# Ternary weights in the convolution stage: the clamp on VectorE replaced by a sign on ScalarE

## The reference, cut to what matters

```
def weight_quant(w):
    s = 1.0 / jnp.clip(jnp.mean(jnp.abs(wf)), EPS, None)
    return (jnp.clip(jnp.round(wf * s), -1.0, 1.0) / s).astype(w.dtype)
```

```
kv = jnp.einsum('bhil,bhjl->bijhl', k_, v_)
y = irfft(rfft(kv, n=2L) * rfft(ssm_kernel, n=2L))[..., :L]
out = y + kv * D
out = jnp.einsum('bijhl,bhil->bjhl', out, q_)
```

## Time and profile before

| | us |
|---|---|
| median of 3 runs | 1134.99 (1133.25 to 1135.4) |
| the profiled execution's own time | 1131.52 |
| its span, first to last instruction | 1129.7 |
| PE busy | 955.3 (85%) |
| DVE busy | 796.1 (70%) |
| ACT busy | 635.8 (56%) |
| POOL busy | 529.4 (47%) |

### The profile page before, as it was taken

One profiled execution on the slowest core, in us unless ns is written; L12 is line 12 of the kernel. 1 busy time (PEld: TensorE's weight loads), 2 busy tenths in 40 slices (PEclk: granted clock), 3 DMA queues, 4 the chain that ended last, 5 costly groups with the idle time before them and its releaser, 6 DMA issues.

```text
span 1129.7 us, 15510 instructions
## 1 busy us (share of the span) xinstructions
PE 955.3 (85%) x5202; PEld 599.6 (53%) x5218; DVE 796.1 (70%) x1319; ACT 635.8 (56%) x1522; POOL 529.4 (47%) x395
## 2 busy tenths in 40 slices
PE   5888795556456665698899999999989999999998
PEld 3666542133122223476667777777765655555554
DVE  4578799778999997778888777778785444332233
ACT  2655493477888834777886777777763232111111
POOL 4222373431699943577777665776654222000000
PEclk8899898669698897999999999999999999999999
DMA  9634001400000000000000332000031000000000
GB/s 336 284 129 150 1 1 34 141 1 1 0 1 0 0 1 0 1 1 1 1 1 1 107 77 75 2 1 1 2 99 33 1 1 1 1 19 1 1 1 19
DMA packets 24223, 43.13 MB, mean 38 GB/s; under 512 B 3600, under 2 KB 19920, under 8 KB 22608
## 3 DMA queue, kind: packets, MB, share of 16 engines
q1 hardware_dynamic: 24144, 42.14, 10.9%
HBM read 41.08 MB, written 1.05 MB: 37 GB/s over the span
## 4 chain that ended last, share of the span: by engine, by line
PE 59%; DVE 17%; POOL 8%; issue 8%; ACT 7%; DMA 0%; DVEq 0%; ACTq 0%; SPq 0%; POOLq 0%
PE ps L2296 13%; PE ps L2317 8%; PE ps L1868 4%; PE ps L1881 4%; PE ps L1827 4%; PE ps L1852 3%; PE ps L1835 3%; ACT ps L2141 3%; POOL wide L1371 3%; POOL arena L1214 3%; PE ps L1860 2%; PE ps L1842 2%; PE ps L2306 2%; PE ps L444 2%; PE ps L484 1%
## 5 line engine op out<-in xcount | busy, mean ns | idle before, releaser
L2335 DVE TENSOR_TENSOR arena<-arena,ps 128x512 f32<-128x512 f32 (+1 forms) x56 | 38.5, 688 | 145.8 <-ACT arena L2328 143.6
L2328 ACT ACTIVATE arena<-ps,arena 128x512 f32<-128x512 f32 (+1 forms) x56 | 38.5, 687 | 155.6 <-PE ps L2296 155.6
L2220 POOL TENSOR_TENSOR arena<-arena 128x4 f32<-128x4 f32 x96 | 98.9, 1030 | 50.6 <-DVE arena L1992 47.9
L2317 PE MATMUL ps<-wide,arena 128*128 128x256 f32 (+1 forms) x448 | 106.3, 380 | 0.0
L2141 ACT ACTIVATE ps<-ps,arena 128x128 f32<-128x128 f32 x256 | 88.4, 354 | 29.4 <-DVE arena L1971 29.2
L2133 ACT ACTIVATE arena<-ps,ones 128x512 f32<-128x512 f32 x96 | 68.2, 787 | 61.5 <-PE ps L1842 61.5
L2317 PEld LDWEIGHTS ps<-wide,arena 128*128 128x128 f32 (+1 forms) x448 | 84.7, 190 | 17.9 <-issue 1.8
L2296 PE MATMUL ps<-XT,wide 128*128 128x512 f16 (+1 forms) x384 | 93.3, 379 | 0.0
L1971 DVE TENSOR_REDUCE arena<-ps 128x4 f32<-128x512 f32 x64 | 43.7, 689 | 54.9 <-PE ps L1852 54.9
L1835 PE MATMUL ps<-wide,arena 128*128 128x512 f16 x256 | 66.8, 397 | 13.7 <-ACT arena L2133 7.2
L1852 PEld LDWEIGHTS ps<-arena 128*128 128x128 f32 x512 | 68.8, 196 | 10.3 <-ACT arena L2133 1.2
(11 more groups left out here) (344 smaller groups left out, 2403.3 us busy)
## 6 DMA issues: line engine op xcount, KB each, us to landing
side<-in_wproj SPq DMA_DIRECT2D x1, 4096.0 KB, 16.7
wide<-in_w_down SPq DMA_DIRECT2D x1, 3584.0 KB, 13.5
side<-in_w_gate SPq DMA_DIRECT2D x1, 3520.0 KB, 18.9
side<-in_w_up SPq DMA_DIRECT2D x1, 3520.0 KB, 12.1
wide<-in_w_gate SPq DMA_DIRECT2D x2, 1728.0 KB, 11.9
side<-in_w_up SPq DMA_DIRECT2D x3, 1024.0 KB, 9.2
arena<-in_taps SPq DMA_DIRECT2D x1, 2048.0 KB, 11.2
wide<-in_wq SPq DMA_DIRECT2D x1, 2048.0 KB, 18.3
```

The costliest lines, as they stand in the source:

```text
L2220: pool.tensor_tensor(rs[:, j, :], var[:, j, :], minus_half[:, j, :], ALU.pow).then_inc(rs_ready, 1)
L2317: last = pe.matmul(self.out(b), self.hid[n % 2][0:m, b * S:(b + 1) * S], self.down[0:m, j, :], start=(j == 0 and b % 2 == 0), stop=(j == M ...
```

## The change

The second pass on ScalarE becomes a sign: Sign(raw - ROUND), written straight to the ternary matrix `flat[n]` in `arena` as bfloat16, and it raises `ternary_ready`. The sign of the rounded integer is the same number as its clamp to -1 .. 1. The bias is now read from a fourth column of `eps`, which one more memset at the start fills. The three clamps on VectorE and the semaphore `rounded` are gone.

```
-        self.eps = self.sb("eps", [P, 3])
+        self.eps = self.sb("eps", [P, 4])
...
         dve.memset(k.eps[:, 1:2], 1e-6)
+        dve.memset(k.eps[:, 3:4], -ROUND)
         dve.memset(k.eps[:, 2:3], LN_EPS * LN_EPS).then_inc(k.eps_ready, 1)
...
-    rounded = k.sem("cv_rounded")
...
-            if CLAMP_AT <= h < CLAMP_AT + 3:
-                n = h - CLAMP_AT
-                dve.wait_ge(rounded, n + 1)
-                dve.tensor_scalar(flat[n], raw[n], 1.0, -1.0, ALU.min, ALU.max).then_inc(k.ternary_ready, 1)
...
             link(act.activation(raw[n], raw[n], ACT.Copy, scale=w_inv[:, n:n + 1], bias=ROUND))
-            act.activation(raw[n], raw[n], ACT.Copy, bias=-ROUND).then_inc(rounded, 1)
+            act.activation(flat[n], raw[n], ACT.Sign, bias=k.eps[:, 3:4]).then_inc(k.ternary_ready, 1)
```

More of the change, by code:

```diff
@@ L660, in gpsimd @@
             w.centre(pool, i)
-    MEAN_AT, CLAMP_AT = 3, 10
+    MEAN_AT = 3
     def vector(dve, link):
```

## The result

The changed kernel takes 1129.16 us, median of 10 runs (1123.32 to 1130.6); the kernel before took 1133.94 in the 10 runs beside it (1130.44 to 1136.82). The ratio is 0.9956, with a 95% interval of 0.9942 to 0.9970, so 5.0 us faster, between 3.4 and 6.6. The forecast was 1128.9 us and 6.1 us faster: the time is met to 0.3 us, the gain was forecast 1.1 us too large.

What follows compares the result with a forecast made beforehand. VectorE's three clamps were taken to lie on the path in the convolution's head loop. Removing them gives 6.1 us, sign hidden, transposes and adds 0: 1134.99 - 6.1 = 1128.9 us, range 1126.2 to 1132.2.

Steps and rivals of the forecast that it cites:

- The clamps are the path: Convolution's head loop: without the clamps heads keep 2.58 us each, so head 15's product comes 6.09 us earlier.
- The value taken: Whole kernel: a gain of 6.1 us, between 4.7 and 6.7.
- the fallen clock of head 15: TensorE's slow matmuls in head 15, at 1.2 GHz: 1.0 us of the 6.1 us gain hangs on them.
- the lower way of reckoning: Head 15's product had the clock not fallen: VectorE busy until 185.21, so a gain of 5.1 us.
- GpSimd and VectorE hold each other up: Head loop, shared ports: a clamp is 1.22 us of work, the rest of its length is waiting for GpSimd.
- The rival of a partial gain: Head loop: only the clamps' own 3.7 us are won, waits return elsewhere, 1131.3 us; chance 0.07.
- The sign is hidden: ScalarE's second pass: three signs of 1.99 us add 0.24 us, covered by its 9.47 us wait for GpSimd.
- The dear sign: Rival on ScalarE: slow signs delay squares and square root, kernel slower from 16.9 us extra; 0.03, shared with other delays.
- Transposes and adds: Stage's end behind head 15, TensorE's transposes and VectorE's adds: change of 0, between - 0.55 and + 0.4 us.
- The clock takes it back: Rival behind the stage: shifted work meets the lower clock, losing 4 us, some 1132.9 us; chance 0.07.

Runs made afterwards that it cites:

- e2: Changed kernel with the sign replaced by a Copy with immediate bias written as bfloat16, no clamps, values left unclamped: 1129.73 us, 0.9968 of before.
- e3: Changed kernel with one of the three clamps back on VectorE after head 10, the other two matrices by sign: 1129.19 us, 0.9970 of before.
- e6: Changed kernel with two of the three clamps back on VectorE after heads 10 and 11, the third matrix by sign: 1128.92 us, 0.9970 of before.
- e1: Kernel before with ScalarE's second pass made a sign, in place in float32, the three clamps kept: 1132.57 us, 1.0005 of before.
- e9: Kernel before once more, unaltered, for a second trace: 1133.81 us, 1.0006 of before.
- e4: Kernel before with all three clamps kept on VectorE but moved out of the loop, behind head 15's sum: 1128.70 us, 0.9961 of before.

## Why the prediction was right

*The clamps are the path; without them the loop keeps 2.58 us a head.* Shown. 6.12 us from the trace that the forecast was made from, for 6.09 forecast, and e2 gets the same loop without any sign. That VectorE cannot pay a clamp back holds for the three together; of a single one it pays back 0.95 us in five heads (e3, e6).

*The value taken, 6.1, between 4.7 and 6.7.* Here the forecast was off by a fifth. The term mis-sized is the fallen clock of head 15: I took the row's value, with 1.0 us that hung on one execution. Two more traces with all three clamps (e1, e9) have no fall and measure 5.05 us, the lower way of reckoning, which I had at 5.1. The prediction named that dependence and chose the wrong end; with three traces, one of which has the fall, it goes with the exception. That the time came out within 0.3 us of 1128.9 all the same is luck: before was at 1134.99 in the three runs that the forecast counts from and at 1133.94 beside the changed kernel, and this 1.05 us cancels the surplus in the gain.

*GpSimd and VectorE hold each other up.* Shown by e3 for GpSimd's side (4.59 us for two kvs beside one clamp) and by e4 for VectorE's: clamps of 1.22 us where GpSimd is idle. The rival of a partial gain (3.7 us, its waits coming back elsewhere) is refuted by the loop, whose waits did not come back, and not by the times, whose interval of 3.4 to 6.6 us has room for 3.7.

*The sign is hidden.* 2.00 us each, for 1.99 forecast. ScalarE's wait shrank from 9.47 to 7.58 us, for "some 8"; the squares ended at 187.1, as worked out, and the square root ran at 188.2, well ahead of the reciprocal at 190.6. e1 shows it in the time too. The dear sign did not happen.

*Transposes and adds: 0, between - 0.55 and + 0.4.* Against the first trace of before the changed kernel's stretch is 0.25 us longer, against the second 0.16 shorter: in the bounds, and around nothing. The lower bound was too narrow: with two clamps the stretch took 5.69 us, 0.8 less than the first trace of before, with no extra work on TensorE.

*The clock takes it back.* I gave this 0.07 for 4 us. Behind the stage the changed kernel is 0.8 us longer than the second trace of before and 1.1 longer than e1's. Of this 0.35 us is VectorE's wait, not the clock. That the rest belongs to the change is argued from two traces of each kernel and not shown.

## What to carry to other kernels

Count the slack a head of a tight loop has before putting side work into it: here 0.2 us a head hid most of one 1.2 us clamp and none of the next, so three cost 5 us where they stood and 1.5 us behind the loop. Where two levels of the clock enter a term, work the sum out at both and take the level that several executions share, not that of the one traced. And compare stage by stage, from a common instruction: whole spans of these kernels moved by several us through what lay ahead of the change.

## What the runs showed of the hardware

- The same gap of 2.10 us on TensorE, behind one of 1.16 us, brought the granted clock to 0.50 in one execution (before, first trace) and left it at 1.00 in two (e1, e9).
- The length of a gap alone did not decide it: with two clamps TensorE idled 2.99 us ahead of the transposes and the clock was still 1.00 from 187 to 188 us; behind 2.57 us in the changed kernel it was 0.50 from 183 us. Three matmul calls in that gap kept it at 1.00 in both executions that had them.
- Sign needed no table load behind Copy and Square, and took 2.00 us for 128x2048 with its bias from a tile, as against 1.91 us for Copy with an immediate bias; writing bfloat16 in place of float32 changed neither (e1, e2).
- A clamp of 128x2048 from float32 to bfloat16 took 1.22 us on VectorE. In the first trace of before the first clamp began at 169.60 us, ahead of a kv at 169.83, and kept its 1.22 us, while two kvs took 4.59 us instead of 3.78; the second began behind a kv and took 2.38, the third behind a centring (177.80 against 177.46) and took 2.63.
